# Layer norm of the last part: one of ScalarE's steps per group is shared out by columns over three engines

## What is computed

```python
out = jnp.einsum('bnm,bmk->bnk', adj, support)      # expert layer
...                                                 # mean, var over all nodes of an expert's graphs
y = (out - m) * inv * bn_gamma[top1][:, None, :] + bn_beta[top1][:, None, :]
x = _layernorm(x + jax.nn.relu(y), axis=-1)         # x is (128, 128, 512)
```

## Time and profile before

| what | value |
|---|---|
| timed executions | 2710.84, 2715.86, 2716.51 us; median 2715.86 |
| the profiled execution | 2712.95 us |
| its span | 2710.9 us |
| busy over the span | TensorE 2573.1 us (95%), VectorE 2106.2 (78%), ScalarE 1782.9 (66%), GpSimd 889.2 (33%) |
| groups' stage of the last part | 2473.70 us (first activation of group 0) to the end |
| last step of ScalarE, line 1455 | 33 instructions, 877 ns mean |
| VectorE's normalising step, line 1517 | 33 instructions, 686 ns mean |
| GpSimd's normalising steps, line 1414 | 62 instructions, 2141 ns mean |

### The profile page before, as it was taken

How to read it: one execution, slowest core, us unless ns; L and a number is a source line. 1 busy time by engine, 2 the same in 40 slices (tenths; PEclk the granted TensorE clock), 3 DMA queues, 4 the chain that set the end, 5 groups by cost and what they waited for, 6 DMA issues and landing times. The chain is left out here.

```text
span 2710.9 us, 61257 instructions
## 1 busy us (share of the span) xinstructions
PE 2573.1 (95%) x20250; PEld 2143.1 (79%) x20250; DVE 2106.2 (78%) x4105; ACT 1782.9 (66%) x6186; POOL 889.2 (33%) x490
## 2 busy tenths in 40 slices
PE   7899999999999999999999999999999999976765
PEld 6788888888888888888888888888888888765654
DVE  5877878778777787777777877878778778775987
ACT  4666666666666666666666666666666666655977
POOL 1133333223233333232332332333323223124876
PEclk9999999999999999999999999999999999988888
DMA  5445445445454454454444544544545445576998
GB/s 216 182 165 189 173 166 193 164 174 191 162 187 176 172 192 165 172 192 160 180 179 170 191 164 181 193 164 175 176 169 187 169 176 187 209 294 251 420 401 316
DMA packets 154765, 538.23 MB, mean 199 GB/s; under 512 B 17554, under 2 KB 50322, under 8 KB 107666
## 3 DMA queue, kind: packets, MB, share of 16 engines
q1 hardware_dynamic: 154514, 534.87, 53.2%
HBM read 425.75 MB, written 109.05 MB: 197 GB/s over the span
## 5 line engine op out<-in xcount | busy, mean ns | idle before, releaser
L826 ACT ACTIVATE prob<-prob,neg_max 128x128 f32<-128x128 f32 x2024 | 782.6, 393 | 5.8 <-DVE abs_max L1014 5.8
L476 POOL TENSOR_TENSOR norm<-norm,constants 128x1 f32<-128x1 f32 x125 | 68.6, 549 | 1402.2 <-DVE norm L1058 1402.2
L826 ACT ACTIVATION_READ_ACCUMULATOR prob<-prob,neg_max 128x1 f32 x2024 | 390.3, 193 | 0.0
L466 POOL TENSOR_TENSOR moments<-moments,conv 128x1024 f32 x122 | 296.0, 2426 | 234.6 <-ACT conv L873 206.4
L812 ACT ACTIVATE qk<-bank 128x512 f32<-128x512 f32 x256 | 152.7, 597 | 319.9 <-PE bank L515 319.9
L986 DVE SCALAR_TENSOR_TENSOR prob<-bank,adj_in 128x512 f32<-128x512 f32 x508 | 314.3, 681 | 11.4 <-PE bank L515 11.4
L1003 DVE TENSOR_TENSOR prob<-prob,inv_sum 128x2048 f32<-128x2048 f32 x126 | 291.0, 2309 | 4.3
L1009 DVE TENSOR_REDUCE neg_max<-prob 128x16 f32<-128x2048 f32 x127 | 289.3, 2278 | 0.0
L1014 DVE TENSOR_REDUCE abs_max<-prob 128x16 f32<-128x2048 f32 x127 | 289.3, 2278 | 0.0
L452 POOL TENSOR_TENSOR xT_lo<-xT_in,xT_hi 128x1024 fp32r<-128x1024 f32 x62 | 274.8, 4432 | 5.0
L819 ACT ACTIVATE probT<-bank 128x512 f32<-128x512 f32 x504 | 260.8, 612 | 14.7 <-PE bank L566 14.5
(11 more groups left out here) (170 smaller groups left out, 5930.3 us busy)
## 6 DMA issues: line engine op xcount, KB each, us to landing
expert_hi<-expert_hi_scratch SPq DMA_DIRECT2D x123, 1024.0 KB, 4.8
expert_lo<-expert_lo_scratch SPq DMA_DIRECT2D x123, 1024.0 KB, 6.9
x_in<-x SPq DMA_DIRECT2D x128, 256.0 KB, 2.7
x_scratch<-x SPq DMA_DIRECT2D x128, 256.0 KB, 2.4
conv_in<-conv_scratch SPq DMA_DIRECT2D x32, 1024.0 KB, 12.2
x_in<-x_scratch SPq DMA_DIRECT2D x32, 1024.0 KB, 10.5
out<-x_in SPq DMA_DIRECT2D x32, 1024.0 KB, 12.8
xT_in<-xT SPq DMA_DIRECT2D x63, 512.0 KB, 3.4
```

The lines of the kernel that those rows point to most:

```text
L466: pool.tensor_tensor(acc, acc, conv[:, :, :].rearrange("p k d -> p (k d)"), ALU.add).then_inc(moments_added, 1)
L826: last = act.activation(prob[:, par2, h, :], prob[:, par2, h, :], ACT.Exp, bias=neg_max2[:, par2, h:h + 1], scale=2.0, accum_out=row_sum[: ...
```

## The change

The normalising of node column 2 (`ACT_TURN`) of groups 0 to 30 is split by columns of the feature axis. ScalarE keeps the first 256 of 512, GpSimd takes 128 as a third instruction at line 1414's place, VectorE takes the last 128 as a second instruction at line 1517's place, directly behind its own. The semaphore counts follow: GpSimd counts 3 a group, VectorE 2. The last group is as before. Nothing else changes: the same bytes are loaded and stored, and the order of each engine's other instructions stays.

```diff
@@ phase_two
     POOL_TURNS, ACT_TURN, DVE_TURN = 2, 2, 3
+    POOL_STEPS, DVE_STEPS = 3, 2
+    ACT_PART, POOL_PART, DVE_PART = slice(0, D // 2), slice(D // 2, 3 * D // 4), slice(3 * D // 4, D)
@@ sync, group
-                sp.wait_ge(pool_finished, (g if ends_here else g + 1) * POOL_TURNS)
-                sp.wait_ge(dve_finished, g + 2 if ends_here else g + 1)
+                sp.wait_ge(pool_finished, (g if ends_here else g + 1) * POOL_STEPS)
+                sp.wait_ge(dve_finished, (g + 1) * DVE_STEPS)
@@ gpsimd, group
-            for j in range(0 if isinstance(g, int) and g == NG - 1 else POOL_TURNS):
-                pool.tensor_scalar(by_node(x1_in, r)[:, j, :], by_node(x1_in, r)[:, j, :], mean_var[:, r % 2, j, 0:1],
+            if isinstance(g, int) and g == NG - 1:
+                return
+            for j, part in ((0, slice(0, D)), (1, slice(0, D)), (ACT_TURN, POOL_PART)):
+                pool.tensor_scalar(by_node(x1_in, r)[:, j, part], by_node(x1_in, r)[:, j, part], mean_var[:, r % 2, j, 0:1],
                                    rstd[:, r % 2, j:j + 1], ALU.subtract, ALU.mult).then_inc(pool_finished, 1)
@@ scalar, group
-                for j in (ACT_TURN, 1) if isinstance(h, int) and h == NG - 1 else (ACT_TURN,):
-                    act.activation(by_node(x1_in, r2)[:, j, :], by_node(x1_in, r2)[:, j, :], ACT.Identity,
+                whole = slice(0, D)
+                for j, part in ((ACT_TURN, whole), (1, whole)) if isinstance(h, int) and h == NG - 1 else (
+                        (ACT_TURN, ACT_PART),):
+                    act.activation(by_node(x1_in, r2)[:, j, part], by_node(x1_in, r2)[:, j, part], ACT.Identity,
@@ vector, finish
-            for j in (DVE_TURN, 0) if isinstance(g, int) and g == NG - 1 else (DVE_TURN,):
-                dve.tensor_scalar(by_node(x1_in, r)[:, j, :], by_node(x1_in, r)[:, j, :], mean_var[:, r % 2, j, 0:1],
+            whole = slice(0, D)
+            for j, part in ((DVE_TURN, whole), (0, whole)) if isinstance(g, int) and g == NG - 1 else (
+                    (DVE_TURN, whole), (ACT_TURN, DVE_PART)):
+                dve.tensor_scalar(by_node(x1_in, r)[:, j, part], by_node(x1_in, r)[:, j, part], mean_var[:, r % 2, j, 0:1],
                                   rstd[:, r % 2, j:j + 1], ALU.subtract, ALU.mult).then_inc(dve_finished, 1)
@@ vector, group
-                    dve.wait_ge(pool_finished, (h - 1) * POOL_TURNS)
+                    dve.wait_ge(pool_finished, (h - 1) * POOL_STEPS)
```

## The result

Six timed executions of the changed kernel took 2723.21 to 2726.86 us, median **2724.8**. Six of the kernel before, beside them, took 2710.84 to 2716.51, median 2712.97. The ratio is 1.0040, 95% interval 1.0029 to 1.0052: slower by more than the 0.2% that a measurement can tell. The loss is 11.8 us, where 6.0 were forecast. The forecast of 2721 came nearer than that only because it was added to a median 2.9 us higher.

The account below looks back on a forecast made before the run. VectorE (6.19 us a group, gapless) and ScalarE (6.17) were taken as tied; VectorE's new 0.65 a group made its pace 6.84, the end 6.0 us late, 2719.0 or 2721.9, forecast 2721, range 2712 to 2727.

Parts of the forecast that it names:

- The step on VectorE: VectorE's new 128-column step, behind GpSimd's second: waits 0.44 us, runs 0.20, rounded to 0.65 a group; pace 6.84.
- beside a busy GpSimd: VectorE's existing 512-column step: said to cost 0.63 us while GpSimd works, against 0.46 alone.
- GpSimd's third step: GpSimd's new 128-column step in groups 0 to 30: 0.52 to 1.03 us, covered by VectorE's pace and charged nothing.
- ScalarE's step: ScalarE's last step, 512 columns cut to 256: 0.70 us becomes 0.45, a gain of 0.25 a group.
- The range: Whole kernel's time: 2712 to 2727 us overall; the forecast's own 2717 to 2726, from 0.45 to 0.85 per step and scatter.
- The sum: Last part, tick by tick: tick 31 at 2709.7 against 2703.72, so the end comes 6.0 us late.
- Tick 12 comes at 2487.36 + 12 x 6.84: VectorE's clock before group 15: tick 12 at 2569.4, the slower pace taking the place of earlier waits.
- the other 24.5 are those waits: Kernel before, 31 ticks: 216.4 us, of which 191.9 at pace 6.19 and 24.5 VectorE's waits for transposes.
- A: Rival: VectorE's new step does not wait for GpSimd, costs 0.20; 2 us less, 2714; chance 0.28.
- B: Rival: ScalarE alone sets the pace, so all 7.8 us of its relief arrive, 2708; chance 0.06.
- C: Rival: VectorE's new step is shut out for GpSimd's whole step, costs 2.1; 39 us more, 2755; chance 0.06.
- D: Rival: GpSimd sets the pace at 6.57 with a cheap VectorE step; some 2717; chance 0.08.

Follow-up runs that it names:

- the pair of added instructions: Kernel before plus one spare-memory instruction behind VectorE's own step: a normalising step of 128 columns, 2728.35 us; or instead a bn_stats of 128 columns, 2715.53 us.
- the odd columns: Changed kernel with VectorE's second step cut to 127 columns and GpSimd given 129: 2726.15 us, ratio 1.0052 to the kernel before.
- the statistics instruction: Kernel before with an extra bn_stats of 128 columns of spare memory behind VectorE's own step: 2715.53 us, ratio 1.0010.

## Why the prediction was right in kind and half in size

*What bounds the kernel: right.* VectorE without a gap, tied with ScalarE. VectorE's half of the split alone makes the loss, GpSimd's half none, and ScalarE's relief is worth nothing.

*The step on VectorE: 0.65 forecast, 0.71 measured.* The wait of 0.44 was right: begun at 0.21 to 0.22, cost 0.71, of which 0.26 is its own, leaves 0.45. What the prediction took for the common price "beside a busy GpSimd", 0.63, belongs to another moment, the end of GpSimd's first step; it entered no term. Too small was "I take 0.20" for 128 columns alone; the trace of before had no small step of this kind. The pace came out as 6.92, not 6.84.

*GpSimd's third step: right*, 0.79 within 0.52 to 1.03, and hidden. *ScalarE's step*: 0.51 (2567.54 to 2568.05 in ScalarE's timeline) where 0.45 was forecast, of no weight. That ScalarE would wait for `shift` before its last step was right too.

*The range.* The measured 2724.8 lies within 2712 to 2727, and within the forecast's own 2717 to 2726, partly by luck. Counted from the median that the forecast stood on, 2715.86, the upper end of that own range is a loss of 10.1 us; the loss was 11.8. From the later median, 2712.97, the same range would have ended at 2723.1.

*The sum: 222.3 from first to last tick forecast (2709.7 - 2487.36), 229.75 measured.* The missing 7.4 us, step by step from the rows above, each event counted from the first tick:

| event | forecast | measured | added on this stretch |
|---|---|---|---|
| group 15 begins | 85.5 | 89.2 | 3.7: twelve ticks by 0.08 are 1.0; 2.7 before tick 8 |
| group 16 begins | 99.5 | 104.5 | 1.3: "14.00 later as before" |
| tick 16 | 114.3 | 119.7 | 0.3 |
| group 23 begins | 145.1 | 150.9 | 0.4: four ticks by 0.08 |
| group 24 begins | 159.5 | 166.5 | 1.2: "14.37 later" |
| tick 24 | 174.4 | 181.3 | 0 |
| tick 31 | 222.3 | 229.75 | 0.5: seven ticks by 0.07 |

Of the three steps that failed the largest is one that I did not write as a term: "Tick 12 comes at 2487.36 + 12 x 6.84 ..., in place of the waits there were before". I let the slower clock swallow every wait before group 15. The one before tick 8 stayed: ticks 7 and 8 are 9.70 apart (2543.75 with 3.54 of idle time before it, against 0.60). There the queue enters its loop and loads the experts of group 8 right before they are needed, and since it stood at the waiting last step, it did so late, 6.6 us behind group 7's first activation instead of 4.6: group 7 to 8 took 10.32 (2516.86 to 2527.18) against 9.01 before. The loads themselves scatter as much (3.1 to 4.5 us there in kernels of the same clock), so the size of this one is partly chance. The second is that the standstills were taken over as they were. I had both halves in hand, that ScalarE would wait for `shift` and that the queue stands behind a waiting instruction, and did not put them together at the jump. The third is the step's own 0.06.

The ticks at 10, 19 and 30, where small waits had stood before (0.9, 0.8 and 2.1 us), came without them, as forecast. One reading of the waits was loose and harmless: "the other 24.5 are those waits" sets the 31 ticks against 31.5 us of waits, of which the longest, 10.5, lies before the first tick.

*The rivals.* A (no wait for GpSimd) fell: in the common group the step waits, in every kernel that has it at this place. That a step can slip in before GpSimd takes hold is true all the same: with ScalarE's groups written out one began at 2538.23, 0.27 behind GpSimd's, cost 0.26, and GpSimd's took 2.40. There VectorE's own step had not been held up before it. B fell, since relief alone won nothing. C fell by the 0.26 in the middle of GpSimd's step. D fell in the changed kernel (0.60 of idle time before the power) and held, with a loss near zero, where only GpSimd took columns.

*What stays open.* Why GpSimd's step holds VectorE in two stretches. Here are only their bounds: the first ends at about 0.50 of GpSimd's step, and at 0.67 (0.22 + 0.45) where that step was itself held up by 0.16; the second goes from about 1.35 to 1.81. That VectorE's rate mode is the cause of the wait is argued from the pair of added instructions, not shown: the odd columns did not leave it, and the statistics instruction differs in what it writes, too (6 columns). What makes an expert load take 0.3 or 1.4 us wasn't tried. The 0.3 us behind the last tick were not followed.

## What to carry to other kernels

Where two engines are tied and one has no gaps, moving work onto it costs all of that work, however small the share, and the relief of the other buys nothing. Price the moved piece where it lands: at the moment at which it will begin, beside what the neighbour runs then, with its fixed part. A price "beside a busy neighbour" is an average over moments: here the same step costs 0.45 or 0.91 by when it begins. And when an engine gets a new wait, go through what its queue would have done ahead of time: a jump or a load that was hidden is uncovered by a wait of 0.7 us.

## What the runs showed of the hardware

- GpSimd's 512-column step (2.07 us) holds up a normalising step of VectorE twice. Begun 0.1 in, 512 columns cost 0.85; 0.7 to 1.33 in, 0.45; 1.36 in, 0.91; 1.65 in, 0.63; from 1.85 on, 0.45. A step of 128 columns begun 0.22 in costs 0.71, begun 0.81 in 0.26. A statistics instruction at 0.22 isn't held up at all (0.19). In the first part of the program the hold lasted to the end, with other instructions: a VectorE one that takes 2.29 us by the median took 4.45 in that group.
- A normalising step of 128 columns costs VectorE 0.26 where 512 cost 0.45: splitting by columns pays the fixed 0.2 again.
- A jump in ScalarE's loop takes its queue 4.9 to 5.7 us here, and the four loads behind it 3.0 to 4.1, while the ring's DMAs run. The queue goes ahead of its engine, but not past an instruction that waits for a semaphore. Letting it jump early won 7 to 8 us, writing the loop out 12 to 14; the second is more than the whole change could have won (7.8).
